# First stage of a state-space and mixture-of-experts kernel: new order of projections, turned rows and exponentials

## The reference, cut to what matters

```python
x = x + xattn(ctx, layernorm(x))     # this part holds the change
x = x + moe_ffn(layernorm(x))        # shared experts and 16 routed ones, top 2

# xattn, for 4 batches of 512 tokens and 512 channels (256 in ctx):
x  = in_proj(ctx)                    # [b, 512 channels, 512 tokens]
u  = silu(conv4(x) + conv_b)         # 4 taps along the tokens
dt_low, Bm, Cm = split(x_proj(u))    # 16 + 16 + 16 rows, called x_dbl
dt = softplus(dt_proj(dt_low) + dt_b)
state = state * exp(dt * A) + (dt * u) * B        # 16 states, scanned over the tokens
y = (sum over states of state * C) + D * u
return swapaxes(y * silu(z))         # z = layernorm(x), channels by tokens
```

## The kernel before

| engine | order before |
|---|---|
| ScalarE | silu_u 0 to 3; conv_again(b+1) 0, 1; silu_z 0; xd_copy; silu_z 1; conv_again 2; silu_z 2, 3; exps 0; conv_again 3; exps 1 to 3; logs 0 to 3 |
| TensorE | z_turn 0; x_dbl; z_turn 1; x_in(b+1, 2); dt_in 0; z_turn 2, 3; dt_in 1; x_in(b+1, 3); dt_in 2, 3; x_in(b+2) 0, 1 |
| VectorE | taps(b+1, 0); total(b-1) 0 to 3; taps(b+1) 1, 2; z_stats(b+1); soft 0; taps(b+1, 3); soft 1 to 3; gap 0 to 3 |

## Time and profile before

### The profile page before, as it was taken

The page is one execution under the profiler, slowest core; times in us unless marked ns, Lnnn a source line. Parts: engine busy times, 40 slices in busy tenths (PEclk is TensorE's granted clock), DMA queues, the critical chain, the costliest instruction groups (busy, mean ns, idle before and its releaser), DMA issues.

```text
span 1049.8 us, 16637 instructions
## 1 busy us (share of the span) xinstructions
PE 899.3 (86%) x4352; PEld 659.5 (63%) x4353; DVE 823.5 (78%) x1347; ACT 529.3 (50%) x995; POOL 748.0 (71%) x466
## 2 busy tenths in 40 slices
PE   5876555778999889988998999889999999998994
PEld 1322334555666566655665556659988899997993
DVE  4788999999999899989999525775798979899000
ACT  3777734445665466646656222025544545554541
POOL 2435899889999799979993101038878788887883
PEclk9897656789999999999999989889999999999996
DMA  5468912552228422562210420154777767674432
GB/s 178 173 268 300 365 60 82 209 211 82 81 74 313 135 80 80 207 223 90 80 60 11 145 75 14 34 173 135 186 203 183 212 177 221 164 231 102 80 60 41
DMA packets 69987, 152.14 MB, mean 145 GB/s; under 512 B 7585, under 2 KB 23969, under 8 KB 64306
## 3 DMA queue, kind: packets, MB, share of 16 engines
q1 hardware_dynamic: 59410, 126.97, 35.1%
q0 software_dynamic: 10528, 24.65, 11.7%
HBM read 112.80 MB, written 38.80 MB: 144 GB/s over the span
## 4 chain that ended last, share of the span: by engine, by line
PE 44%; DVE 26%; issue 16%; ACT 6%; DMA 4%; POOL 3%; DVEq 1%; SPq 1%; ACTq 0%; POOLq 0%
PE bank L666 8%; PE bank L685 6%; PE bank L770 6%; PE bank L772 6%; PE bank L771 6%; DVE bank L1358 6%; DVE gs L1372 5%; PE bank L612 4%; DVE p_acc L1300 2%; DVE e_gu_lo L1521 2%; ACT bank L926 2%; DVE e_gu_hi L1520 1%; PE bank L554 1%; DMA xt<-x_scratch 1%; PE bank L759 1%
## 5 line engine op out<-in xcount | busy, mean ns | idle before, releaser
L1168 POOL TENSOR_TENSOR dbu<-bcs,m_w 128x2048 f32<-128x2048 f32 x64 | 294.3, 4599 | 10.6 <-DVE bank L1358 7.7
L926 ACT ACTIVATE bank<-m_dt,c_a 128x512 f32<-128x512 f32 x256 | 171.0, 685 | 181.8 <-DVE gs L1372 181.7
L1358 DVE TENSOR_TENSOR_SCAN bank<-bank,dbu 128x512 f32<-128x512 f32 x192 | 229.9, 1216 | 16.6 <-issue 8.4
L666 PE MATMUL bank<-ws_gu,f_xnT 128*128 128x352 f32 x576 | 196.0, 482 | 13.9 <-ACT f_hT L948 13.9
L612 PE MATMUL bank<-ident,gs 128*128 128x128 f32 x768 | 130.4, 304 | 57.6 <-DVE gs L1372 48.0
L612 PEld LDWEIGHTS bank<-ident,gs 128*128 128x128 f32 x768 | 97.7, 154 | 107.1 <-DVE gs L1372 78.7
L666 PEld LDWEIGHTS bank<-ws_gu,f_xnT 128*128 128x128 f32 x576 | 108.7, 200 | 63.6 <-ACT f_hT L948 14.9
L770 PE MATMUL bank<-e_gu_hi,e_xT_hi 128*128 x376 | 130.0, 346 | 7.2 <-POOL e_xT_lo L1230 4.3
L1372 DVE TENSOR_TENSOR gs<-bank,bcs 128x512 f32<-128x512 f32 x192 | 127.1, 668 | 0.0
L772 PE MATMUL bank<-e_gu_hi,e_xT_lo 128*128 x376 | 121.9, 324 | 0.0
L771 PE MATMUL bank<-e_gu_lo,e_xT_hi 128*128 x376 | 121.8, 324 | 0.0
(11 more groups left out here) (172 smaller groups left out, 1690.8 us busy)
## 6 DMA issues: line engine op xcount, KB each, us to landing
bcs<-bc_scratch SPq DMA_DIRECT2D x32, 1024.0 KB, 9.0
e_gu<-in_wgu SPq DMA_DIRECT2D x16, 1408.0 KB, 9.2
e_dn<-in_wdn SPq DMA_DIRECT2D x16, 512.0 KB
out_rows<-xt SPq DMA_DIRECT2D x18, 256.0 KB, 2.1
p_x<-in_x SPq DMA_DIRECT2D x4, 1024.0 KB, 7.1
u_scratch<-p_u SPq DMA_DIRECT2D x4, 1024.0 KB, 3.9
silu_z_scratch<-p_sz SPq DMA_DIRECT2D x4, 1024.0 KB, 5.0
dt_scratch<-p_dt SPq DMA_DIRECT2D x4, 1024.0 KB, 4.2
```

Of the source, the lines that this page charges most:

```text
L666: last = mm(dst[:, 0:I], lhs[t], ws_gu[:, t, off:off + I], start=t == 0, stop=t == KH - 1)
L926: f(HS[k % RING_H][:], m_dt[:, q % 2, :], ACT.Exp, scale=c_a[:, q, n:n + 1]).then_inc(exp_done, 1)
L1168: g.tensor_tensor(part_, Bs[:, gr * GRP:(gr + 1) * GRP, :], w, ALU.mult).then_inc(dbu_ready, 1)
L1358: v.tensor_tensor_scan(to, h, dbu[:, n, :], 0.0, ALU.mult, ALU.add).then_inc(scan_done, 1)
```

## The change

The first stage is put in another order, and four smaller things are changed with it.

| engine | order after (b above 0) |
|---|---|
| ScalarE | silu_u 0; conv_again(b+1, 0); silu_u 1 to 3; silu_z 0, 1; xd_copy; silu_z 3; conv_again 1; silu_z 2; exps 0 to 3; conv_again 2; log 0, 1; conv_again 3; log 2, 3 |
| TensorE | z_turn 0; three quarters of x_dbl; z_turn 1; the last quarter; z_turn 3; x_in(b+1, 1); dt_in 0; z_turn 2; dt_in 1 to 3; x_in(b+1) 2, 3; x_in(b+2, 0) |
| VectorE | z_stats(b+1); taps(b+1, 0); total(b-1) 0 to 3; taps(b+1) 1, 2; soft 0 to 3; gap 0, 1; taps(b+1, 3); gap 2, 3 |

In the first batch, `z_stats(0)` comes behind all four taps, GpSimd normalises row tiles 0 and 3 and ScalarE tiles 1 and 2 (`scale_row`), with one small GpSimd multiplication and one small VectorE instruction more. `p_in` is loaded in two halves of the columns. ScalarE calls Silu once on a small tile before anything else. In the last batch u comes before silu(z), and two of the turned rows go to the banks of `x_in`. On the queue of SyncE the loads of the first slot's dt and u stand earlier, and that of the first group of C ahead of the last group of B.

```diff
-            def silu_u(b):
...
+            def scale_row(q):
+                act.wait_ge(norm_made, 1)
+                row = p_x[0][:, q, :]
+                f(row, row, ACT.Identity, scale=p_rs[:, q:q + 1], bias=f_nm[:, q:q + 1]).then_inc(row_scaled, 1)
...
+            act.wait_ge(consts_made, 2)
+            f(p_rs[:], halves[:], ACT.Silu)
             for q in range(DT):
                 conv_first(0, q)
             for b in range(B - 1):
-                silu_u(b)
+                silu_u(b, 0)
                 conv_again(b + 1, 0)
...
+                for q in range(DT):
+                    exps(b, q)
+                conv_again(b + 1, 2)
+                log(b, 0)
+                log(b, 1)
                 conv_again(b + 1, 3)
-                for q in range(1, DT):
-                    exps(b, q)
-                logs(b)
+                log(b, 2)
+                log(b, 3)
...
             for b in range(B - 1):
-                taps(b + 1, 0)
                 if b:
+                    z_stats(b + 1)
+                    taps(b + 1, 0)
                     for q in range(DT):
                         total(b - 1, q)
                 taps(b + 1, 1)
+                if b == 0:
+                    z_stats(1)
                 taps(b + 1, 2)
-                z_stats(b + 1)
-                soft(b, 0)
-                taps(b + 1, 3)
-                for q in range(1, DT):
+                for q in range(DT):
                     soft(b, q)
...
-                for q in range(DT):
-                    gap(b, q)
+                gap(b, 0)
+                gap(b, 1)
+                taps(b + 1, 3)
+                gap(b, 2)
+                gap(b, 3)
...
-            sp.dma_start(p_in[:], inT.rearrange("(t p) n -> p t n", p=P)).then_inc(in_loaded, 16)
+            sp.dma_start(p_in[:, :, 0:2 * P], in_rows[:, :, 0:2 * P]).then_inc(in_loaded, 16)
+            sp.dma_start(p_in[:, :, 2 * P:H], in_rows[:, :, 2 * P:H]).then_inc(in_rest, 16)
```

More of the change, by code:

```diff
@@ L557, in z_turn @@
             def z_turn(b, q):
-                pe.wait_ge(z_norm, b * TB + q + 1)
+                if b == 0 and q in BY_SCALAR:
+                    pe.wait_ge(row_scaled, BY_SCALAR.index(q) + 1)
+                else:
+                    pe.wait_ge(z_norm, b * TB + (q + 1 if b else 2 + q // 3 * 2))
                 final = b == B - 1
@@ L568, in z_turn, with x_dbl @@
                 last.then_inc(z_turned, 1)
-            def x_dbl(b):
-                wait(pe, sz_ready, b * TB + TB * (b == B - 1))
+            def x_dbl(b, between=lambda: None):
+                wait(pe, sz_ready, b * TB)
                 for q in range(DT):
+                    if q == DT - 1:
+                        between()
                     pe.wait_ge(u_ready, b * DT + q + 1)
@@ L588, in _ @@
             for b in range(B - 1):
-                z_turn(b, 0)
-                x_dbl(b)
-                z_turn(b, 1)
+                if b:
+                    z_turn(b, 0)
+                x_dbl(b, between=lambda: z_turn(b, 1) if b else None)
+                if b:
+                    z_turn(b, 3)
+                x_in(b + 1, 1)
+                if b == 0:
+                    z_turn(b, 0)
+                dt_in(b, 0)
+                if b == 0:
+                    z_turn(b, 1)
+                z_turn(b, 2)
+                dt_in(b, 1)
+                dt_in(b, 2)
+                if b == 0:
+                    z_turn(b, 3)
+                dt_in(b, 3)
                 x_in(b + 1, 2)
[L593 to L596, removed]
                 x_in(b + 1, 3)
-                dt_in(b, 2)
-                dt_in(b, 3)
                 if b < B - 2:
                     x_in(b + 2, 0)
-                    x_in(b + 2, 1)
             for q in range(TB):
@@ L857, in conv_again, with silu_u @@
                 conv_first(b, q)
[L859 to L863 removed]
+            def silu_u(b, q):
+                if q == 0:
+                    wait(act, u_stored, b * 16)
+                act.wait_ge(conv_done, b * DT + q + 1)
+                f(p_u[:, q, :], p_acc[:, q, :], ACT.Silu).then_inc(u_ready, 1)
             def silu_z(b, q):
@@ L989, in slot @@
                     if first and n == LOGS_AT:
-                        logs(B - 1)
+                        for k in range(DT):
+                            log(B - 1, k)
                     if rows and q and n == MOMENTS_AT:
@@ L1141, in normalise @@
                 pool.wait_ge(z_rstd, b + 1)
+                if b == 0:
+                    g.tensor_tensor(f_nm[:], f_nm[:], p_rs[:], ALU.mult).then_inc(norm_made, 1)
                 for q in range(TB):
+                    if b == 0 and q in BY_SCALAR:
+                        continue
                     row = p_x[b % 2][:, q, :]
-                    g.tensor_scalar(row, row, p_mv[:, q, 0:1], p_rs[:, q:q + 1], ALU.subtract, ALU.mult).then_inc(z_norm, 1)
+                    g.tensor_scalar(row, row, p_mv[:, q, 0:1], p_rs[:, q:q + 1], ALU.subtract, ALU.mult).then_inc(z_norm, 1 if b else 2)
+                if b == 0:
+                    pool.wait_ge(row_scaled, len(BY_SCALAR))
             for b in range(B):
```

72 lines of the change are left out of this document (44 added, 28 removed).

## The result

The changed kernel takes 1053.41 us (median of 16 runs, 1048.95 to 1060.28), the kernel before 1046.92 on the same chips (16 runs, 1041.69 to 1052.41). The ratio is 1.0061, with an interval of 1.0044 to 1.0078, so the change costs 6.4 us, between 4.6 and 8.2. The forecast was +5.3. The profiled execution of the changed kernel took 1052.59 us, with a span of 1050.9.

The account below looks back on a forecast made before the run. VectorE bounds the scan stage from its start, so the end moves with xd_copy(3). -0.6 (first iteration) + 2 x 2.96 + 0 (last batch) = +5.3 us; 1046.5 + 5.3 = 1051.8 us, range 1047.3 to 1054.5.

Parts of the forecast that it names:

- The iteration, +2.96 each: First stage, b = 1 and 2: softs stand behind the held third taps, so each iteration grows from 24.49 to 27.45 us.
- The steps behind t: Ladder of an iteration from t, the start of silu_u(b, 0), to the next silu of u at t + 27.45.
- The hole: VectorE idle ahead of the third taps in iterations 1 and 2, about 5 us, ended by ScalarE's conv behind the exponentials.
- The first iteration, -0.6: Batch 0: the gains at the start mostly lost behind the softs, so batch 1 starts at 49.05 instead of 49.62 us.
- The half load: Start of batch 0: loading half of p_in first is worth between nothing and 2.3 us, taken as 0.8.
- The small multiplication on GpSimd: Batch 0, behind p_rs on GpSimd: costs between nothing and 1.05 us, taken as 0.5.
- the second rival: TensorE's clock falls in the first iteration too, slowing dt_in and turns by 1.7 us: +7.0, 1053.5 us; chance 0.12.
- The last batch, 0: Last batch of the first stage: xd_copy comes 10.35 us behind the last logarithm, as before.
- The loads, 0: Earlier loads of the first slot gain nothing, as the first scan waits for ScalarE and not for a load.
- The sum: First iteration -0.6, two iterations of 2.96 each, last batch 0: +5.3 us in all.
- TensorE at full clock: Rival: x_dbl of batches 1 and 2 runs at full clock, ladder 1.6 us shorter each: +2.1, 1048.6 us; chance 0.18.
- Faster, VectorE bound: Rival: exponentials end sooner and VectorE's 21.7 us set the iteration: -6.1, 1040.4 us; chance 0.10.

Follow-up runs that it names:

- soft_first: The changed kernel with the four softs of a batch ahead of the third tile's taps on VectorE; 1042.18 us, ratio to the kernel before 0.994.
- soft_behind: totals_first with the softs put back behind the third tile's taps; 1054.01 us in one execution.
- old_last: The changed kernel with the last batch in its old order and banks, silu(z) ahead of u; 1053.64 us.
- old_loads: The changed kernel with the loads of the first slot back in their old places on the queue; 1056.56 us.
- warm_tensor: The changed kernel with four matmuls whose result nobody reads ahead of x_dbl in batches 1 and 2; 1056.46 us.
- totals_first: soft_first with the totals ahead of z_stats and first taps and, in b above 0, four silus of u ahead of conv_again(b+1, 0); 1037.65 us, ratio to before 0.9915.
- rows_gpsimd: The changed kernel with all four rows of the first batch normalised by GpSimd; 1055.66 us.
- no_preload: The changed kernel without the early call of Silu; 1054.06 us.
- preload_alone: The kernel before with only the early call of Silu added; 1044.76 us, ratio to the kernel before 0.9982.

## Why the prediction was right

- **The iteration, +2.96 each.** Measured +3.11 and +2.97. The steps behind t = 49.37: xd_copy at 6.95 (forecast 6.6), exponentials ending at 17.4 (17.2), third taps at 18.06 (18.0), fourth soft at 24.25 (24.1), next t at 27.60 (27.45). The hole is 5.48 and 5.43 (about 5). The cause is shown from both sides: taking the softs out from behind the held taps removes the hole, 8.4 us at `xd_copy(3)` and some 12 of the time (soft_first, ratio 0.994 where the change has 1.0061), and putting them back brings the hole back and sets `xd_copy(3)` 12.0 later (soft_behind). That the iteration came out to within 0.2 has some luck in it, as kernels with the same code in b = 1 have 27.60, 28.06 (old_last) and 27.89 (old_loads).
- **The first iteration, -0.6.** Measured -0.25 (49.37 against 49.62). Two terms were mis-sized and partly cancelled, which is luck, and the rest is less than the scatter of that mark. The half load was worth 0.13 and not 0.8: 4.46 us instead of 4.60, first matmul at 6.04 instead of 6.17. The second half, issued 0.5 later, took 4.7, so the two ran side by side, the case that the prediction had put at nothing. The small multiplication on GpSimd took 0.21 and not 0.5. Dt_in and turns stayed at full clock there, so the second rival did not occur.
- **The last batch, 0.** Measured +0.2. x_dbl took 5.39 for 5.02, and the distance to `xd_copy(3)` grew from 10.35 to 10.57.
- **The loads, 0.** The first scan waited 1.59 us, for ScalarE and not for a load, and with the old queue it came at the same distance.

```profile
111.07 1.23 DVE L1408 TENSOR_TENSOR_SCAN bank<-bank,dbu 128x512 f32<-128x512 f32 x1 [1.59 <-ACT bank L965]
```

- **The sum.** -0.25 + 3.11 + 2.97 + 0.2 = +6.0 at `xd_copy(3)`, and 5.7 of it were left at the last scan: the scan stage hands the shift on, as the earlier trace rows said. The timed runs have +6.4, which the interval does not tell from either, nor from the +5.3 of the forecast. Against the profiled execution the forecast was 1056.9 and 1052.59 came: that comparison failed, because the part behind the last scan took 4.6 us less than in the trace of before.
- **TensorE at full clock** did not occur: the first six records of x_dbl took 4.56, at half clock at first. warm_tensor shows that with a quick x_dbl, and in b = 2 a quick dt_in too, the iteration is 0.4 shorter at most and not 1.6. A kernel with TensorE at full clock throughout was not run.
- **Faster, VectorE bound** did not occur, but its 21.7 was sound: in totals_first the iteration b = 1 is 21.73. The rival asked for exponentials that end at t + 11.5. There ScalarE goes on to the logarithms only at t + 16.4 and VectorE is the bound all the same, so what the rival lacked was another order and not quicker exponentials.

What I had not put a price on is how much of the change's parts work against its loss. The two rows on ScalarE are worth 4.9 at the mark of batch 1, the early table up to 3.4 there, and x_in(b+1, 1) behind x_dbl some 4 in each iteration once the taps are held. As an estimate from these kernels, the change would cost more without them.

**What stays open.** The gains of soft_first and totals_first are larger in the timed runs (6.3 and 8.9 us) than at the mark of `xd_copy(3)` (2.4 and 5.6). At the last scan they are 4.8 and 7.2, which lies inside the intervals of the timed runs. From that mark to the last scan the traces have 467.0 before, 466.6 after, 464.5 in soft_first, 465.4 in totals_first and 464.7 in soft_behind, whose first stage is as long as the changed kernel's. All twelve lie between 464.5 and 467.1, whichever order they have, while the mark itself moves from 102.1 to 121.9. So the stage hands a shift on to within 2.6 us, and the agreement of 6.0 with 5.7 is closer than that by luck. From the last scan to the end, where the code is the same in all, they scatter by 10 us (468.0 to 478.2). No run here separates a small later effect of the order from this.

## What to carry to other kernels

Moving an instruction behind a group on one engine also moves whatever stands behind its consumer on the next engine: ask of each held instruction who queues behind it there, and put the work whose input is already ready in front. A ladder of starts (this step, plus that duration, plus the wait) written from a timeline of one iteration forecast the new iteration to 0.2 us here, while the shares of busy time hardly changed. And a later stage that is bound by one engine hands such a shift on nearly whole, here to within 2.6 us. Read such a shift at a mark inside the trace, because single executions of one kernel differ by more than the change does.

## What the runs showed of the hardware

- TensorE's granted clock fell to half (1.2 of 2.4 GHz) around waits of TensorE, and the price was often paid in another place than the wait. Records of dt_in, x_in or x_dbl took longer in rows_gpsimd (3.78 for 1.98, at 0.50), warm_tensor (4.78 for 2.84, at 0.58), no_preload (eight in 5.37, at 0.68) and preload_alone (x_dbl 6.59 for 5.22, at 0.54). A delay of 1.3 us on ScalarE thus became 3.4 at the mark of batch 1 (no_preload). But a wait does not always cost the clock: in the changed kernel four records behind 1.68 us of waiting took 1.96. The Trainium skill ("TensorE: Matmul & The Clock Gate", HAM oscillation) has a kernel whose bursts of matmuls each start at a lowered clock behind a wait for data. The traces agree in kind: x_dbl behind 4.49 us of idling had a mean clock of 0.60.
- Half of a load was nearly as long as the whole, with the other half under way beside it: the first half of `p_in` took 4.46 us, the second 4.7, the whole 4.60.
- A table load cost ScalarE its 1.28 us and nothing that a row shows behind it.
